# VectorE's side pieces behind a head's six copies and behind the next scan, instead of between the copies, in a two-stream decoder kernel

## The chip, the cores and the metric

The kernel runs on one core of a Trainium2 chip (trn2). The metric is device microseconds of one execution. Engines are named as in the profile: PE is TensorE, DVE is VectorE, ACT is ScalarE, POOL is GpSimd, SP is SyncE.

## The reference

For 16 samples of 256 tokens by 256 features, four sublayers follow each other, each added to x with a tanh gate: attention with contextual positions (CoPE) over a context, a mixture of experts, plain cross attention over the context, and self attention with gated heads. Cut to what matters here:

```
x = x + tanh(g_xattn[0]) * cope_attention(layernorm(x), ctx)      # the "core"
x = x + tanh(g_ffn[0])   * experts(layernorm(x))                  # 8 experts, top 2, and a shared one
x = x + tanh(g_xattn[1]) * cross_attention(layernorm(x), ctx)     # 16 heads
x = x + tanh(g_ffn[1])   * gated_attention(layernorm(x))          # 16 heads, gates over the heads

# cope, for each of 16 heads:
gates = sigmoid(logits)
pos   = min(reversed cumulative sum of gates over the keys, 63)
bias  = interpolate(query @ pos_emb at floor(pos) and ceil(pos))
scores = softmax(logits + bias)
```

## The kernel before

Work is cut by sample. `run_pass(core, rest)` runs in each of its instruction streams two samples at once: the CoPE attention of sample i (the *core*), and the other three sublayers of sample i − 1 (the *side*). There are 17 passes: the first has a core only, fifteen in a hardware loop have both, the last has a side only.

The core loops over steps s = 0 to 18 for 16 heads, software pipelined. Its functions are `core_tensor`, `core_scalar`, `core_pool` and `core_vector`, one for each engine, each with its own fixed order of instructions; semaphores join them. In `core_vector` a step has these parts:

- six masks (L577) of the integer position `shift`, one for each of MOVES = 32, 16, 8, 4, 2, 1
- six predicated copies (L585) in PSUM bank 1, each shifting the table of position slopes by one of the MOVES where its mask is set. Each waits for the one before (semaphore `dve_core`); the first waits for TensorE's table (L381), the last raises `core_moved`, behind which ScalarE copies the result to `slope` (L496)
- `scan(s + 1)`: the cumulative sum of the next head's gates (L554), which waits for ScalarE's gate (L446), then `shift` (L558) and `rises` (L563)
- for head s − 1 the second scan (L603) and the row minimum (L609), behind GpSimd's products

GpSimd's four operations in a step (`steps` L514, `partial` L515, `neg_rest` L521, `partial` L525, all 128x512) wait for the masks of the step and for ScalarE's `slope` of the one before.

The side is a generator on each engine (`side_tensor`, `side_scalar`, `side_pool`, `side_vector`), cut by `yield` into the same 106 pieces on all. Two are taken ahead of the step loop. PIECES says how many belong to each step: 3, 3, 3, 3, 2, 3, 3, 3, 2, 16, 11, 8, 3, 2, 2, 18, 9, 8, 2. FIRST holds two thirds of that (2, 2, 2, 2, 1, 2, 2, 2, 1, 11, 7, 5, 2, 1, 1, 12, 6, 5, 1). TensorE and ScalarE take FIRST[s] pieces at one place of their step and the rest at a later one; GpSimd takes all at the end of its step; VectorE spreads them with `some_pieces(s, n)`: after copy n a sixth of them, and the last sixth behind `scan(s + 1)`. For PIECES[s] = 3 that is one after the second copy, one after the fourth and one behind the scan; for 2 it is one after the third copy and one behind the scan.

VectorE's pieces lie so in the steps:

- step 0: the experts' layer norm; the second half of the split x (L264); routing and `gate_part(0)`
- steps 1 to 6, in turn: `linear_part(e)` with `accumulate(e − 1)` and `gate_part(e + 1)`. Step 1 has linear, gate, linear; step 2 gate, linear, gate; step 3 linear, gate, linear; step 4 gate, linear; step 5 gate, linear, gate; step 6 linear, gate, linear. `gate_part` is L811 twice and L822; `linear_part` is L811 twice, L827, L829, L832; `accumulate` is L838 twice. Between a gate and a linear part ScalarE must run tanh (L755) and the other half's bias copy (L734)
- step 7: the last accumulate, x (L880), and the cross attention's norm
- step 8: keys, values and queries; steps 9 and 10: sixteen row maxima of scores (L1091), then `max_parts` (L1099, L1100), behind which TensorE transposes and ScalarE takes exponentials (L1028); step 11: nothing on VectorE
- step 12: the heads' outputs (L1112, L1113) and x (L891, L892); step 13: the gated attention's norm; keys, values; step 14: normalised queries (L1078, L1080, L1081); step 15: sixteen row maxima, `max_parts`; after it the exponentials, whose end is the pass's tail

Of the kernel before, what the change touches and what calls it, by code (L numbers as in the profile page):

```python
# [47 lines left out]
MOVES = (32, 16, 8, 4, 2, 1)  # L48
# [28 lines left out]
PIECES = [0] * SLOTS  # L77
# [3 lines left out]
FIRST = [(2 * n + 1) // 3 for n in PIECES]  # L81
# [114 lines left out]
def norm_vector(nc, k, dve, step, n, p):  # L196
    sem = k.sem
    for t in range(NT):
        step(nc.vector.bn_stats(n.stats[:, t, :], n.x[:, t, :]))
        step(nc.vector.bn_aggr(n.mean_var[:, t, :], n.stats[:, t, :]))  # L200
    nc.vector.tensor_scalar(n.var[:], n.mean_var[:, :, 1], EPS, None, ALU.add).then_inc(sem[p + "var_ready"], 1)
    dve.wait_ge(sem[p + "rstd_ready"], 1)
    for t in range(NT):
        nc.vector.tensor_scalar(n.xn[:, t, :], n.x[:, t, :], n.mean_var[:, t, 0:1], n.rstd[:, t:t + 1],  # L204
                                ALU.subtract, ALU.mult).then_inc(sem[p + "xn_ready"], 1)
# [54 lines left out]
def second_part(nc, bank, bias, parts, signal):  # L260

    for g in range(NC):
        src = bank[:, g * S:(g + 1) * S]
        nc.vector.scalar_tensor_tensor(parts[:, 1, g, :], src, 0.0 if bias is None else bias[:, g:g + 1],  # L264
                                       parts[:, 0, g, :], ALU.add, ALU.subtract).then_inc(signal, 1)
# [268 lines left out]
def core_vector(nc, k, dve, step, side):  # L534
    sem = k.sem
    dve.wait_ge(sem["core_loads"], 16 * 2 * NT)
    norm_vector(nc, k, dve, step, k.core_norm, "core_")
    dve.wait_ge(sem["core_v_psum"], 1)
    nc.vector.tensor_copy(k.core_v[:, :, 0:D], k.bank[0][:].rearrange("p (t n) -> p t n", t=NT))\
        .then_inc(sem["core_v_ready"], 1)  # L540
    dve.wait_ge(sem["core_k_first"], NC)
    second_part(nc, k.bank[2], k.bk_cope, k.core_k_parts, sem["core_k_second"])
    dve.wait_ge(sem["core_q_first"], NC)
    second_part(nc, k.bank[3], k.bq_cope, k.core_q_parts, sem["core_q_second"])
    next(side, None)
    next(side, None)
    flat = "p t s -> p (t s)"

    def scan(h):
        dve.wait_ge(sem["core_gates"], h + 1)  # L550
        if h >= 1:
            dve.wait_ge(sem["core_rest"], h)
            dve.wait_ge(sem["core_shift_copied"], h)
        step(nc.vector.tensor_tensor_scan(  # L554
            k.c[:].rearrange(flat)[:, ::-1], k.gate[:].rearrange(flat)[:, ::-1],
            k.cap[:].rearrange(flat)[:, ::-1], 0.0, ALU.add, ALU.max))

        nc.vector.tensor_scalar(k.shift[:, :, 0:S], k.c[:, :, 0:S], FLOOR, None, ALU.add)\  # L558
            .then_inc(sem["core_shift"], 1)
        dve.wait_ge(sem["core_shift"], h + 1)  # L560
        if h >= 2:
            dve.wait_ge(sem["core_steps"], 2 * (h - 2) + 1)
        nc.vector.tensor_tensor(k.rises[:, h % 2], k.shift[:, :, 1:S + 1], k.shift[:, :, 0:S], ALU.is_equal)\  # L563
            .then_inc(sem["core_rises"], 1)

    def some_pieces(s, n):

        for _ in range((n + 1) * PIECES[s] // len(MOVES) - n * PIECES[s] // len(MOVES)):
            next(side, None)

    tab = k.bank[1][:].rearrange("p (t s) -> p t s", t=NT)
    scan(0)
    for s in range(H + 3):
        if s < H:
            dve.wait_ge(sem["core_shift"], s + 1)
            for n, b in enumerate(MOVES):
                last = nc.vector.tensor_scalar(k.masks[:, n], k.shift[:, :, 0:S], b, None, ALU.bitwise_and)  # L577
            last.then_inc(sem["core_masks"], 1)
            for n, b in enumerate(MOVES):
                if n == 0:  # L580
                    dve.wait_ge(sem["core_table"], s + 1)
                    dve.wait_ge(sem["core_masks"], s + 1)
                else:
                    dve.wait_ge(sem["dve_core"], moved)
                move = nc.vector.copy_predicated(tab[:, :, 0:S - b], k.masks[:, n, :, 0:S - b], tab[:, :, b:S])  # L585
                if b > 1:
                    moved = step(move, wait=False)
                    some_pieces(s, n)
                else:
                    move.then_inc(sem["core_moved"], 1)  # L590
        else:
            for n in range(len(MOVES) - 1):
                some_pieces(s, n)
        if s + 1 < H:
            scan(s + 1)
        some_pieces(s, len(MOVES) - 1)
        h = s - 1
        if 0 <= h < H:
            dve.wait_ge(sem["core_steps"], 2 * h + 1)
            if h >= 2:  # L600
                dve.wait_ge(sem["core_exp"], NT * (h - 1))
            z = k.z[:, h % 2]
            summed = step(nc.vector.tensor_tensor_scan(z.rearrange(flat)[:, ::-1], k.keep[:].rearrange(flat)[:, ::-1],  # L603
                                                       k.steps[:].rearrange(flat)[:, ::-1], 0.0, ALU.mult, ALU.add),
                          wait=False)
            dve.wait_ge(sem["core_partial"], h + 1)
            dve.wait_ge(sem["dve_core"], summed)
            for t in range(NT):
                nc.vector.tensor_tensor_reduce(  # L609
                    out=z[:, t, :], in0=z[:, t, :], in1=k.partial[:, t, :], scale=-INV_SQRT_HD,  # L610
                    scalar=3e38, op0=ALU.add, op1=ALU.min, accum_out=k.negmax[:, h % 2, t:t + 1])\
                    .then_inc(sem["core_z_ready"], 1)
            dve.wait_ge(sem["core_z_ready"], NT * (h + 1))
# [551 lines left out]
def run_pass(nc, k, core, rest):  # L1165

    sem = k.sem
    with nc.Block() as block:  # L1168
# [39 lines left out]
        @block.vector  # L1208
        def _(dve):
            side = side_vector(nc, k, dve) if rest is not None else iter(())  # L1210
            if core is not None:
                step = stepper(dve, sem["dve_core"])
                core_vector(nc, k, dve, step, side)
            for _ in side:
                pass
            if core is not None:
                core_tail(nc, k, dve, step)
# [401 lines left out]
```

## Time and profile before

| | |
|---|---|
| median of 3 runs | 5772.76 us (5771.01 to 5777.49) |
| the profiled execution | 5764.52 us, span 5762.8 us |
| busy: VectorE | 4173.9 us, 72% of the span |
| busy: TensorE (matmul) | 3495.9 us, 61% |
| busy: ScalarE, GpSimd | 2277.9 us, 40%; 1398.1 us, 24% |
| mean granted TensorE clock | 0.71 of full |
| copies L585 | 1536, 1031.0 us |

The span holds about 200 us of loading and weight preparation with the first pass, then a pass every 346 to 350 us, and a last pass with the side alone. A busy share is an average; which engine's queue sets the pace is read from the timelines of one pass. Times in rows are microseconds from the span's start. In a merged row, "x6" says that six instructions run in a row.

### The profile page before, as it was taken

The numbers are of one execution on the slowest core, as the hardware profiler recorded it, in microseconds if no ns is written. First come the engines' busy times: TensorE is split into PE (matmuls) and PEld (weight loads), VectorE is DVE, ScalarE is ACT, GpSimd is POOL, SyncE is SP. The second block draws the span as 40 slices with busy tenths as digits, with TensorE's granted clock in tenths as the row PEclk, the third lists the DMA queues.
The fourth block names the chain that finished last, engine by engine and source line by source line (L and its number), as shares of the span: only waits on it lengthen the run. The fifth ranks groups of instructions, "written<-read, shape, count | busy, mean of one in ns | idle before, by whom it ended". The sixth has DMA issues, their size and how long they took to land. (4 is left out here: it accounts for less than half of the span.)

```text
span 5762.8 us, 64716 instructions
## 1 busy us (share of the span) xinstructions
PE 3495.9 (61%) x21126; PEld 2255.5 (39%) x21126; DVE 4173.9 (72%) x9130; ACT 2277.9 (40%) x5185; POOL 1398.1 (24%) x1125
## 2 busy tenths in 40 slices
PE   3256575666657566565666656566565665656576
PEld 3133352433425344352433425334352443424353
DVE  3878597685967858597685967858588585967853
ACT  2434344343434434344343443434344343443432
POOL 0423123131222313223122221312223131321310
PEclk7577686766768677686776768677685776867676
DMA  3000000000000000000000000000000000000000
GB/s 114 0 8 1 10 1 1 10 1 10 1 10 1 1 10 1 10 1 1 10 1 10 1 2 8 1 10 1 10 1 1 10 1 10 1 1 10 1 6 2
DMA packets 42741, 41.52 MB, mean 7 GB/s; under 512 B 6468, under 2 KB 42342, under 8 KB 42360
## 3 DMA queue, kind: packets, MB, share of 16 engines
q1 hardware_dynamic: 33144, 28.46, 1.6%
q10 hardware_dynamic: 9216, 8.39, 0.5%
q8 instruction: 189, 3.10, 0.2%
q14 instruction: 192, 1.57, 0.1%
HBM read 32.64 MB, written 4.19 MB: 6 GB/s over the span
## 5 line engine op out<-in xcount | busy, mean ns | idle before, releaser
L663 PE MATMUL banks<-xn,w 128*128 128x256 f16 x6912 | 965.7, 306 | 228.6 <-ACT h L734 228.6
L585 DVE COPY_PREDICATED banks<-masks,banks 128x448 f32<-128x448 int16 (+5 forms) x1536 | 1031.0, 671 | 73.0 <-PE banks L381 12.4
L514 POOL TENSOR_TENSOR steps<-slope,rises 128x512 f32<-128x512 f32 x256 | 295.5, 1154 | 2762.9 <-DVE masks L577 2402.5
L663 PEld LDWEIGHTS banks<-xn,w 128*128 128x128 f16 x6912 | 746.0, 110 | 430.5 <-ACT h L734 253.7
L470 ACT ACTIVATE core_prob<-z,negmax 128x256 f32<-128x256 f32 x512 | 255.9, 503 | 580.7 <-DVE negmax L609 580.6
L554 DVE TENSOR_TENSOR_SCAN c<-gate,cap 128x514 f32<-128x514 f32 x256 | 323.6, 1264 | 182.7 <-ACT gate L446 182.7
L521 POOL TENSOR_TENSOR neg_rest<-shift,c 128x512 f32<-128x512 bf16 x256 | 298.3, 1165 | 463.6 <-DVE masks L577 423.0
L1091 DVE TENSOR_REDUCE row_negmax<-banks 128x2 f32<-128x512 f32 x512 | 337.9, 688 | 72.3 <-PE banks L294 58.8
L294 PE MATMUL banks<-h,eg_eth 64*128 64x256 f16 x1024 | 279.2, 404 | 182.0 <-DVE row_negmax L1091 168.7
L676 PE MATMUL banks<-w,a 128*128 128x256 f32 x1152 | 308.2, 415 | 103.9 <-DVE o L838 66.4
L525 POOL TENSOR_TENSOR partial<-partial,core_scores 128x512 f32<-128x512 f32 x256 | 365.9, 1429 | 1.2
L603 DVE TENSOR_TENSOR_SCAN z<-keep,steps 128x512 f32<-128x512 bf16 x256 | 328.8, 1284 | 40.6 <-issue 38.6
L577 DVE TENSOR_SCALAR masks<-shift 128x512 int16<-128x512 int16 x1536 | 335.4, 290 | 7.8
L515 POOL TENSOR_TENSOR partial<-slope,neg_rest 128x512 f32<-128x512 f32 x256 | 323.9, 1265 | 0.0
L452 ACT ACTIVATE core_scores<-banks,core_offset 128x256 f32<-128x256 f32 x512 | 211.4, 463 | 232.7 <-POOL partial L525 232.3
L218 PE MATMUL banks<-ident,core_prob 128*128 128x128 f32 x1024 | 231.0, 367 | 119.0 <-ACT core_prob L470 119.0
L482 ACT ACTIVATE core_pT<-banks 128x512 f32<-128x512 f32 x256 | 152.8, 597 | 368.4 <-PE banks L218 368.4
L962 PE MATMUL banks<-eg_eth,h 64*128 64x256 f16 x1024 | 228.0, 328 | 109.3 <-ACT more_pT L1028 56.0
L734 ACT ACTIVATE h<-banks,b 128x256 f32<-128x256 f32 x576 | 237.8, 464 | 137.6 <-PE banks L663 137.6
L811 DVE SCALAR_TENSOR_TENSOR u<-banks,b,h 128x256 f32<-128x256 f32 x576 | 250.8, 477 | 52.1 <-PE banks L663 51.0
L676 PEld LDWEIGHTS banks<-w,a 128*128 128x128 f32 x1152 | 228.5, 209 | 144.0 <-DVE a L832 70.6
L218 PE MATMUL banks<-ident,xn 128*128 128x128 f32 x192 | 53.1, 432 | 370.6 <-DVE xn L204 370.6
(254 smaller groups left out, 6875.8 us busy)
## 6 DMA issues: line engine op xcount, KB each, us to landing
stage<-in_L_ffn_w SPq DMA_DIRECT2D x16, 512.0 KB, 5.1
z<-in_ctx ACTq DMA_DIRECT2D x32, 128.0 KB, 2.7
core_pT<-in_x ACTq DMA_DIRECT2D x32, 128.0 KB, 3.1
u<-in_ctx SPq DMA_DIRECT2D x32, 128.0 KB
x<-in_x SPq DMA_DIRECT2D x32, 128.0 KB
out<-x SPq DMA_DIRECT2D x32, 128.0 KB, 1.8
stage<-in_L_ffn_w SPq DMA_DIRECT2D x8, 256.0 KB, 6.7
stage<-in_L_ffn_sw SPq DMA_DIRECT2D x2, 512.0 KB, 4.4
```

The source lines that it names most:

```text
L218: last = nc.tensor.transpose(bank[:, c * S + t * P:c * S + (t + 1) * P], src[:, t, c * P:(c + 1) * P], k.ident[:])
L514: nc.gpsimd.tensor_tensor(k.steps[:], k.slope[:], k.rises[:, h % 2], ALU.mult).then_inc(sem["core_steps"], 1)
L515: nc.gpsimd.tensor_tensor(k.partial[:], k.slope[:], k.neg_rest[:], ALU.mult).then_inc(sem["core_steps"], 1)
L521: nc.gpsimd.tensor_tensor(k.neg_rest[:], k.shift16[:], k.c[:, :, 0:S], ALU.subtract)\
L525: nc.gpsimd.tensor_tensor(k.partial[:], k.partial[:], k.core_scores[:, h % 2], ALU.add)\
L554: step(nc.vector.tensor_tensor_scan(k.c[:].rearrange(flat)[:, ::-1], k.gate[:].rearrange(flat)[:, ::-1], k.cap[:].rearrange(flat)[:, ::-1] ...
L577: last = nc.vector.tensor_scalar(k.masks[:, n], k.shift[:, :, 0:S], b, None, ALU.bitwise_and)
L585: move = nc.vector.copy_predicated(tab[:, :, 0:S - b], k.masks[:, n, :, 0:S - b], tab[:, :, b:S])
L603: summed = step(nc.vector.tensor_tensor_scan(z.rearrange(flat)[:, ::-1], k.keep[:].rearrange(flat)[:, ::-1], k.steps[:].rearrange(flat)[:, ...
L663: last = nc.tensor.matmul(k.bank[bank][:, f * S:(f + 1) * S], w[:, e, a, c, par, f * P:(f + 1) * P], k.x_parts[:, b, c, :], start=(n == 0) ...
L676: last = nc.tensor.matmul(k.bank[7][:, t * D:(t + 1) * D], k.a[:, e % 2, f, t * P:(t + 1) * P], k.w2[:, e, f, :], start=(f == 0), stop=(f ...
L1091: nc.vector.tensor_reduce(k.row_negmax[:, :, h], k.bank[6 + h % 2][:].rearrange("p (t s) -> p t s", t=NT), axis=AX.X, op=ALU.max, negate=T ...
```

## The change

VectorE no longer takes side pieces between the copies. It takes FIRST[s] pieces behind all six, then `scan(s + 1)`, then the rest. No instruction is added or taken away, and the other engines' orders stay.

```diff
-    def some_pieces(s, n):
-
-        for _ in range((n + 1) * PIECES[s] // len(MOVES) - n * PIECES[s] // len(MOVES)):
-            next(side, None)
-
...
                 if b > 1:
                     moved = step(move, wait=False)
-                    some_pieces(s, n)
                 else:
                     move.then_inc(sem["core_moved"], 1)
-        else:
-            for n in range(len(MOVES) - 1):
-                some_pieces(s, n)
+        for _ in range(FIRST[s]):
+            next(side, None)
         if s + 1 < H:
             scan(s + 1)
-        some_pieces(s, len(MOVES) - 1)
+        for _ in range(PIECES[s] - FIRST[s]):
+            next(side, None)
```

## Rows read from the trace of the kernel before

**Rows 1.** The page: busy time by engine; the granted clock in 40 slices.
```profile
PE 3495.9 (61%) x21126; PEld 2255.5 (39%) x21126; DVE 4173.9 (72%) x9130; ACT 2277.9 (40%) x5185; POOL 1398.1 (24%) x1125
...
PEclk7577686766768677686776768677685776867676
```

**Rows 2.** Windows: busy us (x count) by engine, clock, DMA; step 3.
```profile
2158.90:2178.80 19.90, 12.82 (x89) 9.91 (x88) 19.20 (x38) 8.30 (x20) 5.18 (x4) 0.91 0.00 0
```

**Rows 3.** Timeline, VectorE, step 3: start us, us, engine, line, operation [idle before].
```profile
2158.91 1.31 DVE L577 TENSOR_SCALAR masks<-shift 128x512 int16<-128x512 int16 x6
2160.32 1.32 DVE L585 COPY_PREDICATED banks<-masks,banks 128x448 f32<-128x448 int16 x2
...
2163.03 1.64 DVE L829 SCALAR_TENSOR_TENSOR eg_eth<-eg_eth 128x512 f32<-128x512 f32 x1
...
2174.35 0.68 DVE L829 SCALAR_TENSOR_TENSOR eg_eth<-eg_eth 128x512 f32<-128x512 f32 x1
```

**Rows 4.** One line: L829, durations in ns, minimum, median, maximum.
```profile
L829 DVE SCALAR_TENSOR_TENSOR eg_eth<-eg_eth x144: 683/686/1645, 386.0 to 5626.7; 128x512 f32<-128x512 f32 x144
```

**Rows 5.** Timeline, GpSimd, step 3.
```profile
2160.44 1.15 POOL L514 TENSOR_TENSOR steps<-slope,rises 128x512 f32<-128x512 f32 x1 [12.61 <-DVE masks L577]
...
2164.07 1.72 POOL L525 TENSOR_TENSOR partial<-partial,core_scores 128x512 f32<-128x512 f32 x1
```

**Rows 6.** Timeline, VectorE, first pass, where no side work runs.
```profile
156.85 4.21 DVE L585 COPY_PREDICATED banks<-masks,banks 128x448 f32<-128x448 int16 x6
160.97 1.22 DVE L554 TENSOR_TENSOR_SCAN c<-gate,cap 128x514 f32<-128x514 f32 x1
...
179.00 1.98 DVE L554 TENSOR_TENSOR_SCAN c<-gate,cap 128x514 f32<-128x514 f32 x1
```

**Rows 7.** Timeline, VectorE, step 15: a lone copy and what follows.
```profile
2364.38 0.63 DVE L585 COPY_PREDICATED banks<-masks,banks 128x448 f32<-128x448 int16 x1
2364.92 2.08 DVE L1091 TENSOR_REDUCE row_negmax<-banks 128x2 f32<-128x512 f32 x3
```

**Rows 8.** Timeline, VectorE and ScalarE, step 2.
```profile
2144.95 0.64 DVE L822 TENSOR_SCALAR eg_eth<-u 128x512 f32<-128x512 f32 x1
...
2146.16 0.82 ACT L734 ACTIVATE h<-banks,b 128x256 f32<-128x256 f32 x2
...
2148.61 0.48 DVE L811 SCALAR_TENSOR_TENSOR u<-banks,b,h 128x256 f32<-128x256 f32 x1 [1.71 <-PE banks L663]
```

**Rows 9.** Timeline, VectorE and ScalarE, step 0.
```profile
2109.26 0.74 DVE L204 TENSOR_SCALAR xn<-x,side_mean_var,side_rstd 128x256 f32<-128x256 f32 x2 [0.88 <-POOL side_rstd L210]
...
2112.88 0.72 ACT L446 ACTIVATE gate<-gate,half 128x512 f32<-128x512 f32 x1
```

**Rows 10.** Timeline, VectorE, steps 9 and 10.
```profile
2262.34 0.69 DVE L1091 TENSOR_REDUCE row_negmax<-banks 128x2 f32<-128x512 f32 x1 [2.50 <-PE banks L294]
...
2284.93 1.22 DVE L1100 TENSOR_TENSOR small<-row_negmax,small 128x64 bf16<-128x64 f32 x1
...
2293.45 1.23 DVE L554 TENSOR_TENSOR_SCAN c<-gate,cap 128x514 f32<-128x514 f32 x1 [4.54 <-ACT gate L446]
```

**Rows 11.** Timeline, VectorE, step 12.
```profile
2314.26 0.42 DVE L1113 TENSOR_TENSOR o<-banks,rsum 128x256 f32<-128x256 f32 x1
...
2319.96 0.75 DVE L891 SCALAR_TENSOR_TENSOR x<-banks,tanh_g,x 128x512 f32<-128x512 f32 x1 [3.96 <-PE banks L240]
```

**Rows 12.** Timeline, VectorE, step 13.
```profile
2334.28 0.73 DVE L204 TENSOR_SCALAR xn<-x,side_mean_var,side_rstd 128x256 f32<-128x256 f32 x2 [2.02 <-POOL side_rstd L210]
...
2338.10 1.23 DVE L554 TENSOR_TENSOR_SCAN c<-gate,cap 128x514 f32<-128x514 f32 x1 [1.04 <-ACT gate L446]
```

**Rows 13.** Timeline, VectorE and ScalarE, step 14.
```profile
2352.48 1.64 DVE L1081 TENSOR_TENSOR u<-u,temp_row 128x512 f32<-128x512 f32 x1
...
2356.50 0.72 ACT L446 ACTIVATE gate<-gate,half 128x512 f32<-128x512 f32 x1
```

**Rows 14.** Waits by who waited for whom: us in total, times, longest.
```profile
POOL steps L514 <- ACT slope L496: 151.8, 11, 14.6
```

## The prediction

> **What bounds the kernel now.** I read the page first, then VectorE's instruction timeline of one middle pass of the loop (2104 to 2450 us; the other fourteen repeat it within 1 to 3 us), then GpSimd's, ScalarE's and TensorE's in the same stretches. The reader is to see on the page that VectorE is busiest (72%), and TensorE's clock stands at 0.5 to 0.8 of full in the slices [rows 1]. By step of the head loop it is sharper: the stretch of step 3 is 19.90 us with VectorE busy for 19.20 of them [rows 2]. So over most of steps 0 to 15 VectorE's queue sets the pace, and what lengthens or idles it lengthens the pass. After step 15 (about 70 of 347 us, and all of the last pass) there are no copies, and the change touches nothing there. The first pass has no side work, so it doesn't change either. The sum is therefore 15 times one pass.
>
> I count time t from the first mask of a step. Copies begin at t = 1.41 [rows 3]. Two things in that timeline matter.
>
> *Collisions.* L829 took 1.64 us when it lay between the copies, and 0.68 later in the same step, with the same shape [rows 3]; its 144 instances run from 0.683 to 1.645 us [rows 4]. The long ones lie under GpSimd's four operations on steps, partial and neg_rest, which start as the masks end and run from 2160.44 to 2165.79, t = 1.5 to 6.9, undisturbed to about 6.3 [rows 5]. L832 behaves the same, L822 and L827 lose less (their rows, of the same kind, are not shown; nor are those of the smaller waits named below for steps 4, 5, 8 and 15). The copies themselves are not slowed: six in a row take 4.21 us under GpSimd's work [rows 6].
>
> *Cover.* Side pieces wait for TensorE, ScalarE and GpSimd. A copy between two pieces runs in that wait.
>
> **The change, part by part.** No instruction and no DMA is added or removed; VectorE's order alone changes. TensorE, ScalarE and GpSimd keep theirs, and with two thirds of the pieces ahead of scan(s+1) VectorE is in line with what TensorE and ScalarE do with FIRST[s]. No queue of DMAs is passed.
>
> *Joins.* A copy behind a copy must wait for it: six take 4.12 us from start to the start of the scan behind them (160.97 − 156.85) [rows 6]. A lone copy takes 0.54 to 0.59, up to 0.56 here (2364.92 − 2364.38 = 0.54) [rows 7], six lone ones about 3.44. So each new join costs about 0.13: with PIECES 3 three joins become five, +0.25 us (3.87 before); with 2 pieces four become five, +0.14; in steps 9 and 15 all five are new, +0.68. Of the Trainium skill, "VectorE: DVE Perf Modes", section "The DRAIN you can't avoid", says the pipe empties after every operation and that a semaphore between two costs nothing extra. By it the joins cost nothing; the rows differ by 0.13 us each, and the measurement decides.
>
> The pieces now start at t = 1.41 + 4.12 = 5.53, when GpSimd has under 1 us left. By step of the loop:
>
> Steps 1, 3, 6: before, one linear part lay between the copies. L829 and L832 lose 0.95 each and L827 0.08 = 1.98. Now 0.90 us of PSUM work comes first and GpSimd is done. −1.98 + 0.25 = −1.73 each, −5.19.
>
> Step 2: L822 loses 0.21, and there was a wait of 1.71 for TensorE [rows 8]. Both go, but gate_part and linear_part become neighbours: ScalarE's tanh and bias copy now stand open. From L822's end (2145.59) to the first half's h1 (2146.16 + about 0.45) are 1.05 us, where back to back VectorE would start 0.09 before the end: a wait of 1.14. −1.92 + 1.14 + 0.25 = −0.53. Step 5: the same with a wait of 0.86 before: −1.07 + 1.39 = +0.32. In steps 1, 3, 4 and 6 the pair is split by scan(s+1), 2.08 us, which covers the 1.14 (nothing exposed; without that cover 1.14 each).
>
> Step 4: L822 lost 0.79: −0.79 + 0.14 = −0.65. Step 7: nothing but one join, +0.12. Step 8: a wait of 0.65 for the query's first part goes because VectorE comes 2.2 us later: −0.65 + 0.14 = −0.51.
>
> Step 0: the norm's end xn moves from t = 5.7 to 8.6. ScalarE's gate(1) follows xn by 3.6 us (2110.00 to 2113.60) [rows 9]; copies 3 to 6 were in that time, and scan(1) started at 10.16. Now scan(1) waits for the gate until 8.66 + 3.60 = 12.26: +2.10.
>
> Step 9: the reductions L1091 began too early and waited 2.50 [rows 10], and 0.49 later. Now the scores are there at t = 4.5. −2.99 + 0.68 + 0.1 (reductions in a long row keep just ahead of TensorE) = −2.2.
>
> Step 10: max_parts was ready at t = 6.50 (2286.15 − 2279.65), and scan(11) waited from there through transposes and five exponentials, until 2293.45 [rows 10]. Now: 5.53 + 0.60 + about 1.0 = 7.15, everything behind it +0.65. Step 11 has no VectorE pieces: 0.
>
> Step 12: the heads' outputs were ready at t = 3.9 (2314.68), x waits for TensorE's projection till 2319.96 [rows 11], with one copy pair inside. Now they are ready at 6.78, the same 5.35 us pass, and only 1.33 us of copies fewer follow: 2.88 − 1.33 = +1.55.
>
> Step 13: xn was ready at 2335.01 (t = 7.97) after 2.02 us for GpSimd, which was busy with the core, and scan(14) waited for the gate behind it, till 2338.10 [rows 12]. Now var comes at 7.05, GpSimd is free, xn at 8.66: +0.69.
>
> Step 14: L1081 took 1.64 and L1080 1.50 under GpSimd's work; L1081 ended at t = 7.52 and scan(15) came at 12.12. Now q is done at 8.31 (L1078 meets GpSimd's last operation, 1.35 us), the gate 3.10 behind it (2357.22 − 2354.12) [rows 13]: scan at 11.45, −0.65 with rounding.
>
> Step 15: +0.68 for joins. TensorE's transposes for the core sit between scores 11 and 12; a copy hid most of that, 0.29 was left; now 0.59 more. +1.27.
>
> Sum: gains 5.19 + 0.53 + 0.65 + 0.51 + 2.2 + 0.65 = 9.73; losses 0.32 + 0.12 + 2.10 + 0.65 + 1.55 + 0.69 + 1.27 = 6.70. Net −3.0 us per pass, times 15 = **−45 us**. Against the profiled execution (5764.52 us, 5762.8 of them span) that is 5719.5; the median of the runs is 8.2 us above the profiled one, so 5772.8 − 45 = **5728**.
>
> Of the unknown costs, the residual collision is bounded by nothing and by what scan L554 lost in the first pass, where it came at once behind the copies and took 1.98 instead of 1.22 [rows 6]: 0 to 0.76 us in some ten steps, up to 7.6 per pass. I take 0, but for step 14: nearly everywhere a PSUM operation comes first, and those show no collision at all (L811 is 0.47 to 0.49 in all 576). The open handshakes (steps 0, 2, 5, 12, 13, 15) are copied from rows, each to within perhaps 0.5 us: ±1 to 2 us per pass, ±15 to 30 us in all.
>
> **Rivals.**
> 1. *More handshakes open.* In steps 1, 3 and 6 ScalarE's tanh for the piece behind the scan stands behind keep_scores, which waits for GpSimd, and behind the core's transposed probabilities. If that makes VectorE wait as in step 2, 3 × 1.14 us return: net +0.4 per pass, 5779. For: three engines stand in that chain; against: by the timeline ScalarE is free by t = 8 and VectorE reads h1 at 12.3.
> 2. *Slower: GpSimd slides under the pieces again.* GpSimd's start needs slope(s−1), which ScalarE copies behind its own side pieces, and some of its waits end so [rows 14]. L829 now starts at t = 6.77, GpSimd ends at about 6.3 to 6.4. It decides from a start of GpSimd 0.4 us after the masks; with 1.3 us and more L829, L832 lose their 0.95 again. Steps 1, 3 and 6 then save nothing: 5.2 back, net +2.2 per pass, +33, 5806. Against: slope(s−1) comes some 5 us before the step's end in those steps.
> 3. *No effect:* the pace is another engine's, VectorE's gains turn into waits. 5773. Against: 19.20 busy of 19.90 us.
> 4. *Faster:* the handshakes of steps 0 and 12 (3.65 together) overlap with waits that lie there anyway. 15 × 3.0 and about 40 more: 5690.
> 5. *Joins are free,* one empty pipe costing the same whatever follows: the join terms, about 4.1 us per pass, go, −61 us more: 5667. This is the skill's rule above; [rows 6] and [rows 7] speak plainly against it.
>
> **How the numbers follow.** Forecast 5728: 0.62. Rival 1: 0.12. Rival 2: 0.08. Rival 3: 0.07. Rival 4: 0.08. Rival 5: 0.03. A measurement of this kernel can tell about 0.2% (11.5 us) from no change. Faster takes the forecast and rivals 4 and 5: 0.73; same rivals 1 and 3: 0.19; slower rival 2: 0.08. The range runs from 5692 (the forecast with its 30 us and part of rival 4) to 5780 (rivals 1 and 3 whole): it holds about 0.85.
>
> **What would show it.** In the new timeline: copies as one row of 4.21 us in every step; L829, L832, L1080, L1081, L1099 at their short times; waits for the scores before L1091 gone; new waits of 1.1 us before L811 for ScalarE's h in steps 2 and 5, of about 2.4 before L264 in step 0, 5.3 before L891 in step 12, 3.2 before L554 in step 13. Steps 1, 3 and 6 should be 1.7 us shorter, step 0 2.1 us longer. I am wrong if L829 and L832 stay long, if steps 1, 3 and 6 show waits for ScalarE or TensorE, or if TensorE's granted clock in steps 1 to 6 falls, for then its 24 matmuls of one hidden half, in the sum at their present length, would come last.

## The result and the profile after

| | before | after |
|---|---|---|
| median (lowest to highest) | 5771.01 us (5763.65 to 5777.49) | 5757.04 us (5748.72 to 5761.12) |
| the profiled execution | 5764.52 us | 5760.57 us, span 5758.9 |
| busy: VectorE; TensorE | 4173.9; 3495.9 us | 4049.7; 3541.2 us |
| mean granted TensorE clock | 0.712 | 0.695 |

The ratio is 0.9974, with a 95% interval of 0.9963 to 0.9986: 14 us faster by the medians of seven executions. The forecast was 45 us. The two profiled executions lie 4 us apart: that of before is among its fastest, that of after among its slowest. The rows below are theirs. All lines from the change on are five or six lower: L829 is now L823, L822 L816, L811 L805, L1091 L1085, L309 and L318 are as before.

The page of after, busy time and granted clock:

```profile
PE 3541.2 (61%) x21126; PEld 2284.5 (40%) x21126; DVE 4049.7 (70%) x9130; ACT 2258.7 (39%) x5185; POOL 1358.8 (24%) x1125
...
PEclk7567685766768667685766867667685776867676
```

Against [rows 1], VectorE does the same 9130 instructions in 124 us less: the collisions are gone. TensorE does the same 21126 matmuls in 45 us *more*. No matmul was added, so they ran at a lower clock. The mean granted clock, 0.695 against 0.712, says the same. That is the first sign of where the gain went.

Step 3 after the change, VectorE's timeline, then GpSimd's (start us, us, engine, line, operation, idle before):

```profile
2159.15 1.31 DVE L572 TENSOR_SCALAR masks<-shift 128x512 int16<-128x512 int16 x6
2160.56 4.21 DVE L580 COPY_PREDICATED banks<-masks,banks 128x448 f32<-128x448 int16 x6
2164.68 0.87 DVE L805 SCALAR_TENSOR_TENSOR u<-banks,b,h 128x256 f32<-128x256 f32 x2
2165.58 0.43 DVE L821 TENSOR_SCALAR xT<-u 128x512 f32<-128x512 f32 x1
2165.93 0.69 DVE L823 SCALAR_TENSOR_TENSOR eg_eth<-eg_eth 128x512 f32<-128x512 f32 x1
```
```profile
2160.68 1.16 POOL L514 TENSOR_TENSOR steps<-slope,rises 128x512 f32<-128x512 f32 x1 [12.08 <-DVE masks L572]
...
2164.31 1.27 POOL L525 TENSOR_TENSOR partial<-partial,core_scores 128x512 f32<-128x512 f32 x1
```

The copies are one row, GpSimd is done at 2165.58, and L823 starts behind it, at 0.69 us where [rows 3] had 1.64. GpSimd's last operation gained too, 1.27 where [rows 5] had 1.72. All 144 instances of the line are short now ([rows 4] had up to 1645 ns):

```profile
L823 DVE SCALAR_TENSOR_TENSOR eg_eth<-eg_eth x144: 683/685/687, 390.4 to 5622.7; 128x512 f32<-128x512 f32 x144
```

The waits of VectorE, after (who waited for whom: us in total, times, longest):

```profile
DVE c L554 <- ACT gate L446: 265.2, 91, 7.9
DVE x L885 <- PE banks L240: 187.8, 32, 6.3
...
DVE xn L264 <- ACT xn L254: 38.2, 16, 2.4
...
DVE u L805 <- ACT h L728: 35.0, 31, 1.1
...
DVE row_negmax L1085 <- PE banks L294: 22.8, 17, 4.8
```

They are the forecast ones: 2.4 us before L264 (step 0), 1.1 before L805 in steps 2 and 5, 5.7 before L885 in step 12, 3.1 before L554 in step 13. The wait for the cross scores in step 9 is gone; what is left before L1085 lies behind step 15's masks. In the kernel before the five were 182.7, 166.9, 18.6, 1.1 (once) and 58.8 us.

Step by step, each from its masks to the next step's (median over the fifteen passes, us against before), and then from step 15's masks to the next pass:

| step | 0 | 1 | 2 | 3 | 4 | 5 | 6 | 7 |
|---|---|---|---|---|---|---|---|---|
| forecast | +2.10 | −1.73 | −0.53 | −1.73 | −0.65 | +0.32 | −1.73 | +0.12 |
| measured | +2.15 | −1.72 | −0.30 | −1.86 | −0.67 | +0.31 | −1.86 | −0.22 |

| step | 8 | 9 | 10 | 11 | 12 | 13 | 14 | sum 0 to 14 | step 15 and the end |
|---|---|---|---|---|---|---|---|---|---|
| forecast | −0.51 | −2.2 | +0.65 | 0 | +1.55 | +0.69 | −0.65 | −4.30 | +1.27 |
| measured | −0.61 | −1.94 | +0.50 | −0.22 | +1.66 | +1.00 | −0.82 | −4.61 | +4.23 |

So the steps came out 0.3 us better than forecast, and all that is missing lies behind the masks of step 15. That stretch took 88.2 to 89.6 us before, mean 89.0. After, it takes 94 us in eleven of fourteen passes and 90.8 in three, mean 93.24. A gain of 3.0 us a pass was the forecast; 4.23 − 4.61 = −0.38 a pass is what the profiled pair shows, 15 times that is −6, and its two times differ by 3.95.

Two passes of after side by side, the same places of the end in each (28.5, 35.4, 42.3 and 52.4 us behind step 15's masks). First a pass of the 94 us kind, then one of the 90.8 kind (length, busy us and count by engine, granted clock, DMA share, GB/s):

```profile
2039.00:2045.90 6.90, 5.00 (x59) 2.43 (x57) 0.00 (x0) 5.18 (x13) 0.00 (x0) 0.99 0.01 2
2045.90:2052.80 6.90, 5.49 (x38) 2.67 (x35) 0.00 (x0) 3.34 (x6) 0.00 (x0) 0.50 0.00 0
2052.80:2062.90 10.10, 8.60 (x36) 6.38 (x38) 4.54 (x23) 0.83 (x2) 0.00 (x0) 0.50 0.00 0
2735.20:2742.10 6.90, 5.00 (x59) 2.48 (x57) 0.00 (x0) 5.19 (x13) 0.00 (x0) 0.99 0.01 2
2742.10:2749.00 6.90, 4.17 (x45) 2.51 (x42) 1.27 (x4) 3.15 (x6) 0.00 (x0) 1.00 0.00 0
2749.00:2759.10 10.10, 7.28 (x36) 5.11 (x35) 5.07 (x22) 1.21 (x3) 0.00 (x0) 0.66 0.00 0
```

Up to the first boundary both did the same: 59 matmuls, 5.00 us. Then the clock falls to half (1.2 GHz) in one and stays full (2.4 GHz) in the other. TensorE's rows behind it, of the first and of the second pass:

```profile
2049.67 0.64 PE L309 MATMUL banks<-a,v 128*32 128x256 f32 x2 [0.69 <-ACT more_pT L1022]
...
2052.33 1.97 PE L318 MATMUL banks<-ident,u 128*128 128x128 f32 x8 [0.72 <-ACT u L1027]
```
```profile
2744.88 0.41 PE L309 MATMUL banks<-a,v 128*32 128x256 f32 x2 [0.86 <-ACT more_pT L1022]
...
2746.66 1.09 PE L318 MATMUL banks<-ident,u 128*128 128x128 f32 x8 [0.72 <-ACT u L1027]
```

L318 starts 41.9 us behind the masks in the first and 39.9 in the second, and takes 1.97 against 1.09. Up to here this stretch is a chain through TensorE and ScalarE, with VectorE idle, so each such difference lengthens the pass. In the kernel before the same place is at full clock in every pass (from 27 or 28 us behind the masks to 40.6 or later); in the pass of these windows:

```profile
2048.00:2052.00 4.00, 3.05 (x38) 1.63 (x40) 0.00 (x0) 2.88 (x6) 0.00 (x0) 1.00 0.00 0
2052.00:2056.00 4.00, 2.22 (x26) 1.33 (x19) 1.27 (x4) 0.87 (x2) 0.00 (x0) 1.00 0.00 0
```

(its masks of step 15 are at 2015.1, so these are 33 to 41 us behind them).

### The profile page after: what moved, and what is told of

Read it like the earlier page. It is cut to its first block and busy times, and to the rows that moved or that the text cites. A ratio compares the mean times of both kernels' runs of the same rounds, so it can differ in the third digit from the quotient of the medians.

```text
span 5758.9 us, 64686 instructions
## 1 busy us (share of the span) xinstructions
PE 3541.2 (61%) x21126; PEld 2284.5 (40%) x21126; DVE 4049.7 (70%) x9130; ACT 2258.7 (39%) x5185; POOL 1358.8 (24%) x1125
## 5 line engine op out<-in xcount | busy, mean ns | idle before, releaser
L657 PE MATMUL banks<-xn,w 128*128 128x256 f16 x6912 | 940.7, 301 | 187.1 <-ACT h L728 186.0
L657 PEld LDWEIGHTS banks<-xn,w 128*128 128x128 f16 x6912 | 728.6, 108 | 382.1 <-ACT h L728 216.5
L554 DVE TENSOR_TENSOR_SCAN c<-gate,cap 128x514 f32<-128x514 f32 x256 | 324.3, 1267 | 267.8 <-ACT gate L446 265.2
L670 PE MATMUL banks<-w,a 128*128 128x256 f32 x1152 | 329.8, 437 | 77.6 <-DVE o L832 46.6
L1085 DVE TENSOR_REDUCE row_negmax<-banks 128x2 f32<-128x512 f32 x512 | 331.4, 687 | 42.6 <-PE banks L294 22.8
L525 POOL TENSOR_TENSOR partial<-partial,core_scores 128x512 f32<-128x512 f32 x256 | 337.0, 1317 | 1.2
L670 PEld LDWEIGHTS banks<-w,a 128*128 128x128 f32 x1152 | 243.4, 223 | 122.5 <-DVE a L826 50.7
L805 DVE SCALAR_TENSOR_TENSOR u<-banks,b,h 128x256 f32<-128x256 f32 x576 | 251.0, 478 | 53.7 <-ACT h L728 35.0
```

Source lines behind the costliest of these rows:

```text
L525: nc.gpsimd.tensor_tensor(k.partial[:], k.partial[:], k.core_scores[:, h % 2], ALU.add)\
L554: step(nc.vector.tensor_tensor_scan(k.c[:].rearrange(flat)[:, ::-1], k.gate[:].rearrange(flat)[:, ::-1], k.cap[:].rearrange(flat)[:, ::-1] ...
L657: last = nc.tensor.matmul(k.bank[bank][:, f * S:(f + 1) * S], w[:, e, a, c, par, f * P:(f + 1) * P], k.x_parts[:, b, c, :], start=(n == 0) ...
L670: last = nc.tensor.matmul(k.bank[7][:, t * D:(t + 1) * D], k.a[:, e % 2, f, t * P:(t + 1) * P], k.w2[:, e, f, :], start=(f == 0), stop=(f ...
L1085: nc.vector.tensor_reduce(k.row_negmax[:, :, h], k.bank[6 + h % 2][:].rearrange("p (t s) -> p t s", t=NT), axis=AX.X, op=ALU.max, negate=T ...
```

## The experiments

Where an edit has `BEHIND`, it names the steps whose pieces VectorE takes in the new order; the others keep the old one. Where it has none, it is made in the changed kernel or, for e4, in the kernel before. "Steps" is the sum of the changes in steps 0 to 14 of a pass, "end" the time from step 15's masks to the next pass (89.0 in before, 93.24 in after).

**The steps that should gain, alone, and those that should lose.**

```diff
+BEHIND = (1, 2, 3, 4, 6, 7, 8, 9, 11, 14)     # e1_gain_steps
+BEHIND = (0, 5, 10, 12, 13, 15)               # e2_loss_steps
...
+                    if s not in BEHIND:
+                        some_pieces(s, n)
...
+        if s in BEHIND:
+            for _ in range(FIRST[s]):
+                next(side, None)
```

> VectorE's new order only in steps 1, 2, 3, 4, 6, 7, 8, 9, 11 and 14; the other steps as in the kernel before. Theory (steps add up, as in the prediction): these steps save 1.73 x 3 + 0.53 + 0.65 + 0.51 + 2.2 + 0.65 - 0.12 = 9.6 us per pass, 15 times 144 us: about 5627, less or more by what TensorE's clock does at the end of a pass (up to 3 us per pass, 45 us). Rival (the steps are coupled, what one saves is waited for in the next old step): under half of it, above 5700.

> The complement: the new order only in steps 0, 5, 10, 12, 13 and 15. Theory: they cost 0.32 + 2.10 + 0.65 + 1.55 + 0.69 + 1.27 = 6.6 us per pass, 99 us: about 5870, give or take 45 us for the clock. Rival: with coupling, the two complements do not add up to the whole change's -14 us once the clock's share is taken out.

e1: 5624.63 us (5620.45 to 5629.41), ratio 0.9742 (0.9726 to 0.9758). Steps −9.46, end 88.5 to 89.1 (three of its fifteen passes have a longer step 11, see below). e2: 5898.45 us (5886.06 to 5899.51), 1.0211 (1.0194 to 1.0228). Steps +5.91, end 90.3 to 93.8. The first lies 2 us from its expectation, the second 28 above its own, most of it in the end. The two step sums give −3.55, the whole change −4.61, so they add within 1.1. Of that, 0.84 is step 5: e1 leaves it in its old order behind a shorter step 4, and it takes 0.84 us more than before, while its new order, in after and in e2, takes 0.31 more. So the per-step accounting holds, and steps 0, 10, 12, 13 and 15 were a loss. Step 5 was one against the kernel before, but beside e1 its new order is 0.5 us the better one.

**A few more matmuls in the end.** Twenty matmuls of 64x256 behind scores of five late heads of the gated attention, into a free bank; nothing reads them.

```diff
+        if kind == "gated" and k.both and 9 <= h <= 13:
+            pe.wait_ge(sem["core_scores_copied"], (NT + 1) * H)
+            for _ in range(4):
+                nc.tensor.matmul(k.bank[0][:, 0:S], k.keys[0:64, 0, 0:P], k.queries[0:64, 0, :], ...)
```

> The changed kernel with four extra matmuls (64x256, into bank 0, which nobody reads any more) behind the transposed scores of heads 9 to 13 of the gated attention, 20 per pass, in passes with both streams. Theory (the missing gain is TensorE's granted clock, which fell to half at 35.3 us after the masks of step 15 in 11 of 14 passes and made those 3 us longer than the other three): the clock stays full to at least 42 us, every pass takes about 345.2 us instead of 348.1, so about 33 us less than the changed kernel: 5724. Rival (the tail is longer because of its order, not of its clock): no gain, or a few us lost by 20 more matmuls of 0.11 to 0.21 us: 5757 to 5785.

> The same extra matmuls in the kernel before, where the clock was full at that place (27 to 41 us or longer after the masks of step 15). Theory: little to win, 0 to 10 us less (in 8 of 14 passes the clock dipped from 41 to 48 us, behind most of the tail's matmuls); 5760 to 5772. Rival (extra matmuls help or hurt by themselves): the same difference as between e3 and the changed kernel.

In after (e3): 5720.51 us (5716.59 to 5722.43), 36.5 us less than after, ratio to before 0.9911 (0.9894 to 0.9927). In before (e4): 5769.85, ratio 0.9996 (0.9987 to 1.0006). The steps of e3 are those of after (−4.56); the end is 90.2 to 90.8 in *every* pass. The same three stretches of e3:

```profile
2022.50:2029.40 6.90, 5.71 (x71) 3.59 (x73) 0.00 (x0) 5.23 (x13) 0.00 (x0) 1.00 0.01 2
2029.40:2036.30 6.90, 4.83 (x56) 2.78 (x48) 0.92 (x4) 3.26 (x6) 0.00 (x0) 1.00 0.00 0
2036.30:2046.40 10.10, 6.18 (x36) 3.94 (x36) 5.42 (x23) 1.21 (x3) 0.00 (x0) 0.83 0.05 16
```

Added work made the kernel faster, and only the one whose clock had fallen. Besides the twenty matmuls and a wait that guards their bank nothing was changed, so most of the missing gain was the clock.

**Step 15 back to the old order.**

```diff
+BEHIND = (0, 1, 2, 3, 4, 5, 6, 7, 8, 9, 10, 11, 12, 13, 14)     # e5_undo15
```

> The changed kernel with step 15 alone put back to the old order. Steps 0 to 14 keep their sum (-4.6 us per pass against before). The end of the pass (masks of step 15 to the next pass's first masks) was 94.0 us in 11 of 14 passes of the changed kernel, 90.8 in three, 89.2 before. Theory (step 15's own order costs about 1.5 us, 0.68 for joins, 0.6 for scores that TensorE gives later, and its length also sets where TensorE's clock falls): the end takes 89 to 89.5 in all passes; 5757 - 15 x 4.6 + a few = about 5695. Rival (the clock falls there because of what steps 0 to 14 do, whatever step 15 does): about 1.5 us per pass, 5735.

5718.64 us (5716.66 to 5720.41), ratio 0.991 (0.9894 to 0.9927): 38 us less than after. Steps −3.93, end 89.0 to 91.4. It lies between the two expectations, and both parts are in it. `max_parts` ends 16.88 us behind the masks in before, 18.75 in after and 17.29 here, so step 15's own order cost 1.5 us a pass (22 us). The end as a whole is 3.4 us shorter than in after, and the rest of that is clock, which isn't as long at full as in before in every pass (91.4 us in one). The 0.4 us that `max_parts` is still late is a wait of 0.52 us before step 15's first copy, which is there in e5 too: it comes from the order in the steps ahead.

**GpSimd put under the pieces again.** GpSimd's `steps` waits for the last copy instead of the masks.

```diff
-                pool.wait_ge(sem["core_masks"], s + 1)
+                pool.wait_ge(sem["core_moved"], s + 1)
```

> The changed kernel, with GpSimd's four operations of a step waiting for the last copy (core_moved) instead of the masks: they start at 5.6 us after the first mask instead of 1.5 and run under the side pieces. Theory (the gain of steps 1, 3 and 6 was GpSimd's work no longer lying under L829 and L832): those are long again, 1.6 us for 0.69, and step 1, 3 and 6 are longer by 2 us or more, with some 0.7 us in steps whose scan L554 now meets GpSimd too: 10 to 16 us per pass and about 40 in the first, 5950 within 60. Rival (they were long because of the copies beside them, or because of TensorE's evictions): L829 stays at 0.69 us and the steps stay, 5757 to 5800.

6287.4 us (6281.76 to 6290.15), ratio 1.0894 (1.0875 to 1.0913). Of this kernel, L823's durations, its waits and the scan's row by line:

```profile
L823 DVE SCALAR_TENSOR_TENSOR eg_eth<-eg_eth x144: 681/1747/1754, 459.1 to 6154.8; 128x512 f32<-128x512 f32 x144
```
```profile
DVE c L554 <- POOL neg_rest L521: 192.0, 59, 4.0
```
```profile
L554 DVE TENSOR_TENSOR_SCAN c<-gate,cap 128x514 f32<-128x514 f32 x256 | 385.5, 1506 | 456.0 <-ACT gate L446 236.7 <-POOL neg_rest L521 192.0 <-issue 25.2
```

The same instruction takes 1.75 us under GpSimd's work and 0.685 without it, now in the new order. The collision is a matter of when, not of which order. The page "GPSIMD Engine Reference" of the Trainium skill, section 1 (Specifications), says that GpSimd's SBUF interfaces are shared with VectorE and that instructions with two SBUF inputs contend; L823 is one of those, and the trace agrees. The time was 337 us above the expectation's middle. Much of that is a coupling that it left out: scan(s + 1) may not overwrite `c` before GpSimd has read it for `neg_rest`, and now waits up to 4.0 us for that, 192 us in all, besides being slowed itself (mean 1506 ns against 1267, 61 us over its 256 instances).

**The open pair covered.** In steps 2 and 5 the gate part goes back behind the fourth copy; the rest is as in after.

```diff
+                    if n == 3 and s in (2, 5):
+                        next(side, None)
...
-        for _ in range(FIRST[s]):
+        for _ in range(FIRST[s] - (s in (2, 5))):
```

> The changed kernel with the gate part of steps 2 and 5 moved ahead to behind the fourth copy, so that copies 5 and 6 lie between it and the linear part. Theory (the 35 us that VectorE waits before L805 for ScalarE are the handshake that the copies used to cover): the waits of 1.1 us go or fall under 0.4, one join less; against it L816 meets GpSimd's last operations. Steps 2 and 5 shorter by 0.3 to 1.1 us each, 9 to 33 us in all, 5724 to 5748, if TensorE's clock does not answer. Rival (ScalarE's chain is late by itself): the wait stays, only moved.

5736.08 us (5726.94 to 5737.14), ratio 0.9937 (0.9918 to 0.9955). Steps 2 and 5 are 1.28 shorter each than in after, and the wait for ScalarE's h is gone. That is 38 us; the kernel got 21. The end kept its clock in more passes and gave another 15 us (mean 92.2 against 93.2), but step 11 took 14.6 to 14.7 us in twelve of fifteen passes, where after has 12.1 to 12.5 in all: 29 us lost. Step 11 has no pieces for VectorE and no instruction that was moved.

**Putting it together.** e8 takes the new order in the steps that gain and in 5, with e3's extra matmuls. e9 takes the same steps with e7's pair, and no extra matmul.

```diff
+BEHIND = (1, 2, 3, 4, 5, 6, 7, 8, 9, 11, 14)     # both
```

> The new order in steps 1 to 9, 11 and 14, the old one in 0, 10, 12, 13 and 15, and the extra matmuls of e3. Step 5 in the old order took 17.5 us in e1 (behind a shorter step 4), 17.0 in the new order in the changed kernel: 0.5 us per pass better than e1, 8 us; the extra matmuls nothing, since e1's pass ends took 88.9 us with no dips: 5617. Rival: the step behind takes the gain of step 5 back, 5625.

> The steps of e1 and step 5 in the new order, with the gate part of steps 2 and 5 behind the fourth copy as in e7. By steps: e1's 9.5 us per pass, 0.5 for step 5 and 2 x 1.3 for the pair: 12.5 us per pass, 188 us, 5583, if step 11 takes 12.2 us. Theory: that step and the end of the pass depend on when TensorE's clock rises (12.2 to 12.5 us where it rose 14.4 to 15.6 us into step 10, 14.6 to 14.7 where it rose at 17.3 to 17.8), which this kernel doesn't control: 5583 or up to 37 us more, 5620. Rival (e8's step 11 was longer because of its fill matmuls): step 11 takes 12.2 us, no passes at 14.7.

e8: 5665.39 us (5659.99 to 5667.36), 0.9818 (0.9801 to 0.9835), a miss of 48. Step 5 came out at +0.31 as wanted, but step 11 takes 14.7 us in twelve of fifteen passes (median +2.27), and the end has a mean of 90.0 where e1 without the extra matmuls had 88.9. Against e1 that is 24 and 17 us. In e8's end the clock falls at 41 us behind the masks in most passes, in e1 at 48, so the extra matmuls don't hold it everywhere. e9: **5598.83 us (5590.88 to 5604.83), 0.9705 (0.9689 to 0.9721), the best version**, 169 us below the kernel before as timed beside it, within its expectation. Steps −11.74, with step 11 at +0.49 (12.1 to 13.0 in nine passes, 14.5 to 14.7 in six) and the end at 88.2 to 91.0. It has the long step 11 without any extra matmul, as e1 and e7 have, so these aren't what makes it. Its step 5 on VectorE:

```profile
2136.80 2.76 DVE L586 COPY_PREDICATED banks<-masks,banks 128x448 f32<-128x448 int16 x4
2139.47 0.87 DVE L822 SCALAR_TENSOR_TENSOR u<-banks,b,h 128x256 f32<-128x256 f32 x2
2140.37 0.50 DVE L833 TENSOR_SCALAR eg_eth<-u 128x512 f32<-128x512 f32 x1
2140.78 1.41 DVE L586 COPY_PREDICATED banks<-masks,banks 128x508 f32<-128x508 int16 x2
2142.59 0.88 DVE L822 SCALAR_TENSOR_TENSOR u<-banks,b,h 128x256 f32<-128x256 f32 x2 [0.40 <-PE banks L674]
```

Two copies run while ScalarE makes h. The gate part reads PSUM for one of its inputs and suffers little under GpSimd (0.87 and 0.50 here, 0.87 and 0.43 in the clear).

Why step 11 has two lengths, read in e1, which has both. The first two windows cover step 11 of one pass, the last three that of a later one:

```profile
1231.00:1241.00 10.00, 5.92 (x68) 3.11 (x60) 7.31 (x16) 8.54 (x21) 4.73 (x4) 0.99 0.00 1
1241.00:1243.20 2.20, 2.14 (x18) 0.73 (x18) 2.02 (x7) 0.63 (x3) 0.00 (x0) 0.50 0.03 7
2586.50:2592.60 6.10, 4.58 (x52) 2.46 (x54) 4.31 (x11) 5.68 (x14) 3.27 (x3) 0.99 0.01 1
2592.60:2596.00 3.40, 3.40 (x25) 1.52 (x18) 0.91 (x2) 1.09 (x3) 1.47 (x2) 0.52 0.00 0
2596.00:2601.10 5.10, 2.58 (x26) 0.82 (x22) 4.08 (x9) 3.77 (x8) 0.00 (x0) 0.82 0.02 3
```

The first of them lasts 12.2 us with the clock full for ten of them. In the later one it drops to half for 3.4 us in the middle, with TensorE busy all that time, and the step lasts 14.6.

What goes with it is when the clock last rose in step 10. In all kernels but e6, 180 passes, step 11 took 12.0 to 13.1 us in all 125 passes where that rise came 2.0 us or more before step 11's first mask, and 14.4 to 14.7 in all 55 where it came 1.7 us or less before it. Before and after have one and none of the long ones. e7 shortened steps 2 and 5 alone by 1.28 us each, and twelve passes tipped over. Why the rise comes where it does, no run shows.

**Raising the clock ahead of step 11.** e9 with 36 gapless matmuls in front of the cross attention's transposes, and e3's extra ones: e10 with weights and data on 64 partitions, e11 on all 128.

```diff
+    if kind == "cross" and k.both:
+        for _ in range(36):                      # e11: k.core_keys[:, ...], k.core_queries[:, ...]
+            nc.tensor.matmul(k.bank[5][:, 0:S], k.core_keys[0:64, 0, 0:P], k.core_queries[0:64, 0, :], ...)
```

> e9 with 36 extra matmuls (64x256, bank 5, free there) while TensorE idles 8.8 us in step 10 for max_parts of the cross attention, and the 20 of e3 at the end of a pass. Theory: TensorE comes to the exponentials at its full clock, step 11 takes 12.2 us in every pass, and step 10, whose first transposed scores ran at the half clock, is shorter by up to 1 us: 5560 to 5583, with little spread between runs. Rival (the clock there is not moved by such work, or the extra matmuls are in the way of the transposes): 5590 and above.

> e10 with the 36 extra matmuls of step 10 over all 128 rows of the array instead of 64 (128x256, the same number, place, bank and length). In e10 they ran without a gap for 7.9 us right ahead of the exponentials' transposes, and the granted clock stayed at half through them and for 7 us behind. Theory A (matmuls over half the rows count for less in what raises the clock): now it rises during the 36 or right behind them, the exponentials of steps 10 and 11 run at full clock, step 11 takes 12.2 us and step 10 up to 1 us less; 5560 to 5580. Theory B (the rise comes too late for other reasons, whatever the rows): as e10, 5605 within 12.

e10: 5605.45 us (5603.31 to 5613.27), 0.9724 (0.9708 to 0.974). e11: 5615.2 us (5614.48 to 5616.43), 0.9737 (0.9721 to 0.9753). Of one pass, the stretch of the 36 matmuls and what follows, e10 and then e11:

```profile
1200.20:1208.10 7.90, 7.90 (x40) 5.18 (x35) 7.52 (x19) 1.09 (x4) 3.59 (x4) 0.50 0.01 2
1208.10:1215.00 6.90, 4.28 (x27) 2.00 (x30) 3.88 (x5) 2.81 (x6) 1.13 (x1) 0.50 0.00 0
```
```profile
1202.30:1206.50 4.20, 4.20 (x21) 3.02 (x21) 3.92 (x13) 1.09 (x4) 0.36 (x1) 0.50 0.01 4
1206.60:1213.40 6.80, 3.12 (x29) 2.15 (x28) 6.59 (x11) 1.21 (x3) 4.26 (x4) 0.98 0.00 0
1213.40:1220.20 6.80, 6.80 (x50) 3.18 (x50) 3.14 (x5) 3.99 (x8) 0.00 (x0) 0.52 0.00 0
1220.20:1227.00 6.80, 4.79 (x52) 2.60 (x52) 5.05 (x15) 6.22 (x15) 2.41 (x3) 0.97 0.00 1
```

Over 64 partitions, 7.9 us of it left the clock at half, in every one of the fifteen passes; it rose 8.9 us or more behind them. Over 128 it rose while they ran, in every pass: 4.6 us after they began in this one, 2.4 to 4.6 in all. Step 10 is 1.08 us shorter than before for it (0.21 in e10, 0.22 in e9, which has no extra matmuls). But it fell again at 1213.7, just where the exponentials' matmuls come, and step 11 takes 14.4 to 14.7 us, which costs 2.1. Neither beats e9: the 16 to 39 us below e9 that were expected weren't there.

## Why the prediction was right and wrong

*Collisions: right.* Steps 1, 3 and 6 forecast −1.73, measured −1.72, −1.86 and −1.86; e6 shows the cause by bringing it back. Rival 2 (GpSimd slides under the pieces) didn't happen: its `steps` starts 0.22 us after the masks end in step 3, and all 144 instances of L823 are short. Steps 4, 8 and 14 came within 0.17, step 9 within 0.26. One reading behind it was thin: in the first pass, by which the prediction says that GpSimd doesn't slow the copies [rows 6], GpSimd works for 1.1 us of their 4.2. The changed kernel shows it properly, with GpSimd busy from 2160.68 on and the six copies still at 4.21.

*Joins: right.* Six copies in a row take 4.12 us from their start to the next instruction's wherever that one is ready (2160.56 to 2164.68), where six lone ones were about 3.44. Rival 5 would have taken about 4 us more off a pass; the steps came out 0.3 us below the forecast. Step 7, forecast +0.12 for one join, was −0.22: in before its first copy waited 0.46 us, in after 0.1, and the prediction had no term for that.

*Open handshakes: right.* Steps 0, 5 and 10 are within 0.15 us, step 12 within 0.11, step 2 within 0.23, step 13 0.31 above. e7 shows those of steps 2 and 5 by closing them, 1.28 us each. Rival 1 (the same in steps 1, 3 and 6) is out, since those steps are 1.72 to 1.86 shorter. So is rival 4 (the handshakes of steps 0 and 12 overlap with waits): both cost what was forecast. Rival 3 named 5773, near the 5757 that came out, but its mechanism, gains of VectorE that turn into waits, isn't what the steps show.

*Additivity: right* within 1.1 us in 4.6, by e1 and e2.

*The step that failed* is the term of step 15, +1.27 with everything behind it merely shifted, and with it the sentence "After step 15 (about 70 of 347 us, and all of the last pass) there are no copies, and the change touches nothing there." Up to `max_parts` step 15 took 1.87 us more, 0.6 more than forecast. Its own order cost 1.45, which e2 shows alone (18.33 against 16.88 us to the end of `max_parts`); the other 0.42 is a new wait for TensorE's table before the first copy, here in VectorE's timeline of step 15 of after:

```profile
2012.31 4.21 DVE L580 COPY_PREDICATED banks<-masks,banks 128x448 f32<-128x448 int16 x6 [0.52 <-PE banks L381]
```

Behind that, the same matmuls run at another clock: 3.1 us more in eleven passes of fourteen, 2.36 as a mean. 15 × 2.36 = 35 us, and 15 × 0.6 = 9 us, less 15 × 0.3 = 5 us that the steps gave more: 39 or 40 of the 41 us that lie between the forecast (−45) and the profiled pair (−4). The three passes that kept the clock take 345.2 to 345.3 us against a mean of 347.7 before; had all done so, the forecast would have promised 0.6 us a pass too much and no more. The prediction named TensorE's clock as what could make it wrong, but looked for it in steps 1 to 6, where TensorE's work is hidden, and not in the end of the pass, where TensorE is the chain. The durations that it carried over from before were durations at full clock.

*What stays open.* In the two passes of after the clock rises at the same place, 28.5 and 28.6 us behind the masks, the activity up to the boundary is the same to 0.1 us, and yet it falls at 35.3 us in one and at 42.2 in the other. So the rows don't tell what decides. e3, e5 and e11 moved or filled the work ahead; no run shifted it alone, by a known fraction of a microsecond.

## What to carry to other kernels

Filler between dependent instructions has two sides: it covers a handshake, and it may meet another engine on a shared memory path. Decide for each place by its own rows; here ten steps gained 9.5 us a pass from moving it, steps 0, 5, 10, 12 and 13 lost 5.9 and step 15 1.5 more. The choice by step gave 2.6%, and 3% with the pair of steps 2 and 5 covered, where the uniform rule gave 0.3%. Where a stretch of the chain lies on TensorE, look up the granted clock there, pass by pass and not as a mean: a stretch 1.9 us longer ahead of it went with 3 us lost behind, and no sum of instruction times at the old clock can show that. TensorE's busy time rising at an unchanged count of matmuls is the sign on the page.

## What the runs showed of the hardware

- Passes of one loop, with the same instructions, take one of two lengths by the granted clock alone: 94.0 or 90.8 us in the end of after; 12.0 to 13.1 or 14.4 to 14.7 in step 11, over twelve kernels.
- Extra matmuls can save time: twenty small ones a pass took 36.5 us off one kernel (e3), nothing off another (e4), and in a third (e8) the end took 90.0 us with them, where e1's took 88.9 without.
- 36 gapless matmuls over 64 partitions (7.88 us) left the clock at half; over 128 partitions it rose 2.4 to 4.6 us after they began. Only these two bursts were compared.
- `scalar_tensor_tensor` on 128x512 f32 with two SBUF inputs: 0.685 us, or 1.75 under GpSimd's `tensor_tensor`; GpSimd's own went from 1.72 to 1.27 without it.
